# A fused attention and product-key expert kernel: W_up kept in SBUF, one-hots in rings of 64-token blocks, and the four gate blocks in one stage behind queries, picks and scores

## Chip, cores and metric

One core of one Trainium2 chip. The metric is the device time of one execution in microseconds (us), lower is better. Before the change it is 3835.45 us, the median of three runs (3822.84 to 3841.05).

## What is computed

Input is x of 2 sequences x 4096 tokens x 256 features, float32. An attention-like layer comes first (running sums over the sequence, gates, a layer norm and a projection), then a product-key mixture of experts with 8 heads:

```python
x = x + _layernorm(_L0_attn_ref(_layernorm(x), ...))
...
q = (x @ Wq + bq).reshape(B, S, 8, 64)          # x is the layer norm of the line above
s1, s2 = q1 @ K1.T, q2 @ K2.T                   # 64 scores each, per head
v1, i1 = top_k(s1, 10); v2, i2 = top_k(s2, 10)
vals, best = top_k(v1[..., :, None] + v2[..., None, :], 10)
expert_idx = i1 * 64 + i2 at best               # 10 experts per head, of 64 x 64
h = gelu(x . W_down[expert_idx]) * softmax(vals)
out = sum over heads and experts of h * W_up[expert_idx]
x = x + _layernorm(out)
```

The change touches the second phase alone.

## The kernel before

The first phase (`attention_phase`) writes x1 to DRAM. The second (`experts_phase`) works on 32 chunks m of C = 256 tokens. It does not gather experts. It computes x . W_down for all 4096 experts, multiplies by a matrix of gates that is zero where an expert was not chosen, and multiplies by W_up. An expert's number is split into q (0 to 127) and r (0 to 31), and the gates of one token are the product of two one-hot matrices over its 80 slots (8 heads x 10): `ohq` (80 x 128) and `ohr` (80 x 32), the second scaled by the gate in a high and a low half.

Every engine has its own program, a loop over m from -3 to 32 in which stages of four chunks are interleaved by hand. Semaphores join the engines. The loop body m of each engine:

- **TensorE (PE)**: `gate_matrix(m)` (line 1044): 16 fills of a PSUM bank, 32 matmuls each, in four blocks of 64 tokens; then for p = 0 to 18 `down(m, p)` (line 1117, x times W_down for 256 experts, 12 matmuls) and `up(m, p - 3)` (line 1128, 4 matmuls, listed as 8), with `turn_gates(m + 1)` at p = 4 and `turn_x(m + 3)` at p = 16; then `queries(m + 3)` (line 1092), `sum_picks(m + 2)` (1067), `scores(m + 3)` (1102), `turn_picks(m + 2)` (1074). Gates, queries and scores share three PSUM banks in rotation (`fills`, `fill`).
- **ScalarE (ACT)**: `keep_gates(m)` copies the gate banks to SBUF (1162); then per p the `gelu` of the down results (1258) and four rows of the fourth block's one-hot (`distances`, `near`: 1237, 1245); then `turn_x`, `queries`, `turn_picks`, `scores`, and `soften(m + 2)`, an exponential between two table loads (1218, 1221).
- **VectorE (DVE)**: moments, `decode(m + 1)` (expert numbers to q and r), the top-10 lists of chunk m + 2 (`lists_first`, `lists_rest`, `pair_sums`, `pairs_top`, `pick`), then `low_gates`, `onehots(m + 1, 0)`, `onehots(m + 1, 1)`, `finish(m)` (1346, statistics of the output; waits for the last `up`), `onehots(m + 1, 2)`, `norm_out(m)` (1362), `onehots(m + 1, 3)`. One block of one-hots is an ohr compare (1306), for blocks 0 to 2 an ohq compare (1312), and two ohr products (1318, 1320).
- **GpSimd (POOL)**: `mix(m, p)`, the product of gelu and gates (1002), between `down` and `up`; `low_x` (976), reciprocal roots (983, 986), `add_input` (991).
- **SyncE (SP)**: issues every DMA. Per p a load of 512 KB of W_down, split in two parts beforehand (`load_down`, 946, three slots), and one of 256 KB of W_up (`load_up`, 952, four slots).

Each one-hot of a chunk has a place of its own, so block b waits for the matmuls of the same block one chunk earlier. The ring of loads on SP waits like this:

```python
def load_down(m, p):
    n = m * PAIRS_R + p
    if n >= WD_SLOTS:
        sp.wait_ge(down_pe, n - WD_SLOTS + 1)
...
def load_up(m, p):
    n = m * PAIRS_R + p
    if n >= 4:
        sp.wait_ge(up_pe, n - 3)
```

Before the loop the kernel splits W_down into the two parts, in 16 pieces (`high_down` on ACT, line 1251, `low_down` on GpSimd, 996) and stores them in DRAM (`keep_parts`, 924 and 927).

Of the kernel before, what the change touches and what calls it, by code (L numbers as in the profile page):

```python
# [9 lines left out]
P = 128  # L10
D = 256
# [7 lines left out]
C = 256  # L19
# [13 lines left out]
WD_SLOTS = 3  # L33
# [759 lines left out]
def experts_phase(nc, ctx, sems, chunks, x1_dram, out_dram, w, x1_written):  # L793
# [16 lines left out]
    wup = sb("b_wup", [P, 4, 2, D], F32)  # L810
# [29 lines left out]
    ohq = sb("b_ohq", [SLOTS, C, NQ], F16)  # L840
    ohr = sb("b_ohr", [SLOTS, C, 2, NR], F16)
# [176 lines left out]
    def pe_program(pe):  # L1018
# [13 lines left out]
        def gate_matrix(m):  # L1032
            for g in range(GROUPS):
                if g % BLOCK_GROUPS == 0:
                    if g // BLOCK_GROUPS == BLOCKS - 1:
                        pe.wait_ge(ohq_act_done, ACT_PARTS * (m + 1))
                    else:
                        pe.wait_ge(ohq_done, (BLOCKS - 1) * m + g // BLOCK_GROUPS + 1)
                    pe.wait_ge(ohr_lo_done, BLOCKS * m + g // BLOCK_GROUPS + 1)
                bank = fill(("gates", m, g))  # L1040
                for n in range(GROUP):
                    tok = g * GROUP + n
                    for part in range(2):
                        mm = T.matmul(bank[:, n * NR:(n + 1) * NR], ohq[:, tok, :], ohr[:, tok, part, :],  # L1044
# [572 lines left out]
```

## Time and profile before

| | |
|---|---|
| median of three runs | 3835.45 us |
| the profiled execution, its own time | 3823.96 us |
| span of its profile, first to last instruction | 3822.2 us |
| mean granted TensorE clock | 0.903 |
| PE busy | 3296.1 us, 86% |
| DVE busy | 3301.0 us, 86% |
| ACT busy | 2118.1 us, 55% |
| POOL busy | 1554.4 us, 41% |
| DMA | 486.93 MB, mean 127 GB/s |

The experts' phase begins at about 797 us. Its first gate matmul starts at 969.4 us, the last at 3751.2. Shares are of the whole span. Rows of groups of instructions give line, engine, operation, output<-inputs, shapes and count, then busy time and the mean of one in ns, then the engine's idle time just before them and what ended it. Matmuls overlap, so the durations of single ones add up to more than the time they take.

### The profile page before, as it was taken

Reading aid. Unit: us, or ns where it says so; the run is one execution under the profiler, and the core shown is the slowest. Engines: PE = TensorE matmul, PEld = TensorE weight load, DVE = VectorE, ACT = ScalarE, POOL = GpSimd, SP = SyncE. Lnnn points to the kernel's source line nnn. Section 1 sums busy time; section 2 is a strip of 40 time slices with the busy share of each in tenths; the row PEclk is TensorE's granted clock in tenths of the full one; section 3 lists DMA queues with packets and bytes.
Section 4 is the critical chain, followed back from the end, with each engine's and each line's share of the span. In section 5 each row is a group of like instructions: output and inputs, shape, how many; then the busy total and the mean of one; then the engine's idle time right before and its main releaser. Section 6 shows DMA issues by size and latency. Waiting matters only on the chain.

```text
span 3822.2 us, 91364 instructions
## 1 busy us (share of the span) xinstructions
PE 3296.1 (86%) x31732; PEld 2774.3 (73%) x31732; DVE 3301.0 (86%) x15276; ACT 2118.1 (55%) x4379; POOL 1554.4 (41%) x990
## 2 busy tenths in 40 slices
PE   5999999922799898998999899998988898988887
PEld 4666666511688788887877888887888887877777
DVE  4566666529999999999999999999999999999961
ACT  3444444414556666666666666655666666666662
POOL 1334343330244444444444444444443444444443
PEclk9999999966899988899998989999988989999988
DMA  1111111140344444444444444444444444444443
GB/s 60 56 50 50 57 55 50 34 157 34 111 159 142 142 156 142 142 157 157 155 158 144 158 150 158 150 156 142 143 154 142 150 150 156 157 152 155 152 168 136
DMA packets 205910, 486.93 MB, mean 127 GB/s; under 512 B 22041, under 2 KB 69785, under 8 KB 203164
## 3 DMA queue, kind: packets, MB, share of 16 engines
q1 hardware_dynamic: 205452, 481.08, 36.5%
q8 instruction: 255, 4.18, 0.4%
q14 instruction: 203, 1.66, 0.1%
HBM read 439.03 MB, written 25.17 MB: 121 GB/s over the span
## 4 chain that ended last, share of the span: by engine, by line
PE 62%; issue 8%; ACT 3%; POOL 1%; DVE 1%; DMA 1%; POOLq 0%; DVEq 0%
PE b_ps_a L1128 22%; PE b_ps_h L1117 21%; PE b_ps_s L1044 10%; PE b_ps_m L1067 3%; PE b_ps_s L1102 3%; PE b_ps_s L1092 3%; POOL b_hid L1002 1%; ACT L1221 1%; DMA b_wd_split<-wd_parts 1%; ACT b_score L1212 0%; ACT b_gates L1162 0%; DVE b_ohq L1312 0%; ACT L1218 0%; PE b_ps_m L1057 0%; ACT b_gate L1218 0%
## 5 line engine op out<-in xcount | busy, mean ns | idle before, releaser
L1002 POOL TENSOR_TENSOR b_hid<-b_hid,b_gates 128x512 f32<-128x512 f32 x512 | 897.5, 1755 | 1264.4 <-ACT b_hid L1258 1264.2
L1117 PE MATMUL b_ps_h<-b_xT_hi,b_wd_split 128*128 128x256 f32 x4096 | 898.7, 305 | 212.1 <-issue 206.7
L1128 PE MATMUL b_ps_a<-b_wup,b_hid 128*128 128x256 f32 x4096 | 968.1, 382 | 1.8 <-POOL b_hid L1002 1.6
L1117 PEld LDWEIGHTS b_ps_h<-b_xT_hi,b_wd_split 128*128 128x128 f32 x4096 | 710.5, 203 | 313.3 <-issue 308.8
L1128 PEld LDWEIGHTS b_ps_a<-b_wup,b_hid 128*128 128x128 f32 x4096 | 751.7, 192 | 90.7 <-POOL b_hid L1002 4.2
L1258 ACT ACTIVATE b_hid<-b_ps_h 128x512 f32<-128x512 f32 x512 | 304.7, 595 | 647.2 <-PE b_ps_h L1117 647.0
L1237 ACT ACTIVATE b_ohq<-b_q_no,b_minus_qid 80x128 f16<-80x128 f16 x2048 | 648.3, 391 | 1.0
L1117 PE MATMUL b_ps_h<-b_xT_lo,b_wd_split 128*128 128x256 f32 x2048 | 603.5, 295 | 0.0
L1044 PE MATMUL b_ps_s<-b_ohr,b_ohq 80*128 80x32 f16 x16384 | 448.2, 185 | 84.9 <-ACT b_gates L1162 54.7
L1044 PEld LDWEIGHTS b_ps_s<-b_ohr,b_ohq 80*128 80x128 f16 x16384 | 439.7, 102 | 92.0 <-ACT b_gates L1162 57.8
L1312 DVE TENSOR_TENSOR b_ohq<-b_qid,b_q_no 80x8192 f16<-80x8192 f16 x96 | 449.5, 4682 | 0.0
L1117 PEld LDWEIGHTS b_ps_h<-b_xT_lo,b_wd_split 128*128 128x128 f32 x2048 | 417.7, 204 | 1.6
L1162 ACT ACTIVATE b_gates<-b_ps_s 128x512 f32<-128x512 f32 x512 | 298.4, 596 | 143.8 <-PE b_ps_s L1044 141.8
L1245 ACT ACTIVATE b_ohq<-b_ohq,b_one 80x1024 f16<-80x1024 f16 x256 | 291.5, 1139 | 0.1
L1318 DVE TENSOR_TENSOR b_ohr<-b_ohr,b_ghi 80x2048 f16<-80x2048 f16 x128 | 247.6, 1935 | 1.1
L237 POOL TENSOR_TENSOR a_ret<-a_prod 128x512 f32<-128x512 f32 x64 | 85.0, 1328 | 324.2 <-DVE a_prod L615 324.2
L1320 DVE TENSOR_TENSOR b_ohr<-b_ohr,b_glo 80x2048 f16<-80x2048 f16 x128 | 202.3, 1580 | 4.4
L1394 DVE FIND_INDEX8 b_idx<-b_val,b_score 128x8 uint16<-128x64 f32 x1024 | 200.4, 226 | 0.0
L1379 DVE FIND_INDEX8 b_idx<-b_val,b_score 128x8 uint16<-128x64 f32 x1024 | 200.3, 227 | 0.0
L1386 DVE MATCH_REPLACE8 b_score<-b_val,b_score 128x64 f32<-128x64 f32 x1024 | 199.8, 220 | 0.0
L1067 PE MATMUL b_ps_m<-b_work,b_ident 128*128 128x160 f16 x864 | 143.3, 342 | 48.3 <-DVE b_work L1488 48.3
L477 ACT COPY a_carry<-a_ps_c 32x512 f32<-32x512 f32 x128 | 68.0, 577 | 210.8 <-PE a_ps_c L333 210.5
(186 smaller groups left out, 5321.6 us busy)
## 6 DMA issues: line engine op xcount, KB each, us to landing
b_wd_split<-wd_parts SPq DMA_DIRECT2D x512, 512.0 KB, 3.6
b_wup<-in_wup SPq DMA_DIRECT2D x512, 256.0 KB, 2.7
a_keysh<-a_key SPq DMA_DIRECT2D x16, 896.0 KB, 5.4
a_x<-in_x SPq DMA_DIRECT2D x16, 512.0 KB, 4.7
x_between<-a_y SPq DMA_DIRECT2D x16, 512.0 KB, 3.2
b_x<-x_between SPq DMA_DIRECT2D x32, 256.0 KB, 2.7
wd_parts<-b_wd_split SPq DMA_DIRECT2D x16, 512.0 KB, 2.7
b_x1t<-x_between SPq DMA_DIRECT2D x32, 256.0 KB, 4.6
```

The costliest lines, as they stand in the source:

```text
L1002: G.tensor_tensor(hid[:, p % 4, :, :], hid[:, p % 4, :, :], gates[:, 2 * p:2 * p + 2, :], ALU.mult).then_inc(mix_done, 1)
L1044: mm = T.matmul(bank[:, n * NR:(n + 1) * NR], ohq[:, tok, :], ohr[:, tok, part, :], start=part == 0, stop=part == 1)
L1067: mm = T.matmul(rows, ident16[:, :], pk[:, :, c, :], start=c == 0, stop=c == NPAIR - 1)
L1117: mm = T.matmul(hbank[p % 2][:, j * C:(j + 1) * C], a, c, start=i == 0, stop=i == len(parts) - 1)
L1128: mm = T.matmul(abank[:, t * D:(t + 1) * D], hid[:, p % 4, j, t * P:(t + 1) * P], wup[:, p % 4, j, :], start=p == 0 and j == 0 and t == 0, ...
L1162: S.mul(gates[:, :, g * GROUP:(g + 1) * GROUP], sbank[fills["gates", m, g] % 3][:, :].rearrange("p (n r) -> p r n", r=NR), 1.0 / GATE_SCAL ...
L1237: op = S.activation(ohq[:, C - BLK + i, :], q_no[0:SLOTS, :], ACT.Abs, bias=minus_qid[:, i:i + 1])
L1245: S.activation(rows, rows, ACT.Relu, bias=one[:, :], scale=-1.0).then_inc(ohq_act_done, 1)
L1258: S.activation(hid[:, p % 4, :, :], hbank[p % 2][:, :].rearrange("p (j c) -> p j c", j=2), ACT.Gelu).then_inc(gelu_done, 1)
L1312: V.tensor_tensor(ohq[:, tok, :].rearrange("p n (q s) -> p n q s", s=2), qid[:, tok, :].unsqueeze(2).to_broadcast(shape_q), q_no[0:SLOTS, ...
L1318: V.tensor_tensor(hi, lo, ghi[:, tok, :].unsqueeze(2).to_broadcast(shape), ALU.mult).then_inc(ohr_hi_done, 1)
L1320: V.tensor_tensor(lo, lo, glo[:, tok, :].unsqueeze(2).to_broadcast(shape), ALU.mult).then_inc(ohr_lo_done, 1)
```

## The change

W_up stays in SBUF (`wup` holds all 32 r), loaded once; `load_up` is gone. There are four slots for W_down in place of three. `ohq` has three places of 64 tokens in place of the whole chunk: blocks 0 and 2 share place 0, block 1 has place 1, block 3 (made by ACT) has place 2. `ohr` has two places, for even and odd blocks. `gate_matrix` and `keep_gates` work by block, and the four blocks of chunk m + 1 stand at the end of loop body m.

```diff
-WD_SLOTS = 3
+WD_SLOTS = 4
...
-    wup = sb("b_wup", [P, 4, 2, D], F32)
+    wup = sb("b_wup", [P, NR, D], F32)
...
-    ohq = sb("b_ohq", [SLOTS, C, NQ], F16)
-    ohr = sb("b_ohr", [SLOTS, C, 2, NR], F16)
+
+    ohq = sb("b_ohq", [SLOTS, 3, BLK, NQ], F16)
+    ohr = sb("b_ohr", [SLOTS, 2, BLK, 2, NR], F16)
...
+    def place(b):
+        return 2 if b == BLOCKS - 1 else b % 2
...
             sp.dma_start(wdown, w["wdown"].rearrange("(k p) r q -> p k r q", p=P)).then_inc(wdown_in, 16)
+            sp.dma_start(wup[:, :, :], w["wup"]).then_inc(wup_in, 16)
...
-                    load_up(m, p)
...
-        def gate_matrix(m):
-            for g in range(GROUPS):
-                if g % BLOCK_GROUPS == 0:
-                    if g // BLOCK_GROUPS == BLOCKS - 1:
-                        pe.wait_ge(ohq_act_done, ACT_PARTS * (m + 1))
-                    else:
-                        pe.wait_ge(ohq_done, (BLOCKS - 1) * m + g // BLOCK_GROUPS + 1)
-                    pe.wait_ge(ohr_lo_done, BLOCKS * m + g // BLOCK_GROUPS + 1)
+        def gate_matrix(m, b):
+            if b == BLOCKS - 1:
+                pe.wait_ge(ohq_act_done, ACT_PARTS * (m + 1))
+            else:
+                pe.wait_ge(ohq_done, (BLOCKS - 1) * m + b + 1)
+            pe.wait_ge(ohr_lo_done, BLOCKS * m + b + 1)
+            for g in range(b * BLOCK_GROUPS, (b + 1) * BLOCK_GROUPS):
...
             pe.wait_ge(mix_done, n + 1)
-            pe.wait_ge(wup_in[p % 4], 16 * (n // 4 + 1))
+            pe.wait_ge(wup_in, 16)
...
         for m in range(-3, chunks + 1):
-            if has(m):
-                gate_matrix(m)
             for p in range(PAIRS_R + LAG):
...
             if has(m + 2):
                 turn_picks(m + 2)
+            if has(m + 1):
+                for b in range(BLOCKS):
+                    gate_matrix(m + 1, b)
...
             if has(m + 3):
                 scores(m + 3)
+            if has(m + 1):
+                for b in range(BLOCKS):
+                    keep_gates(m + 1, b)
             if has(m + 2):
                 soften(m + 2)
...
-            if m:
-                dve.wait_ge(gates_pe, GROUPS * (m - 1) + BLOCK_GROUPS * (b + 1))
+            if n >= 2:
+                dve.wait_ge(gates_pe, BLOCK_GROUPS * (n - 1))
```

PE runs the same matmuls in the same order: what stood first in body m + 1 now stands last in body m. DVE's order is the same too, with another number to wait for ahead of line 1306. Two queues change their order.

SP, the middle of one chunk's loads (`b_wd_split` are the slots of W_down, `b_wup` those of W_up, `b_down_pe` and `b_up_pe` PE's counts). Before:

```order
L946 DMA b_wd_split<-wd_parts 128x1024 [waits b_down_pe]
L952 DMA b_wup<-in_wup 128x512 [waits b_up_pe]
L921 DMA b_x<-x_between 128x2x256 [waits a_x1_out,b_xT_pe]
L946 DMA b_wd_split<-wd_parts 128x1024 [waits b_down_pe]
L952 DMA b_wup<-in_wup 128x512 [waits b_up_pe]
L946 DMA b_wd_split<-wd_parts 128x1024 [waits b_down_pe]
L952 DMA b_wup<-in_wup 128x512 [waits b_up_pe]
L940 DMA out<-b_y 128x2x256 [waits b_res]
```

After:

```order
L924 DMA b_x<-x_between 128x2x256 [waits a_x1_out,b_xT_pe]
L950 DMA b_wd_split<-wd_parts 128x1024 [waits b_down_pe] x2
L944 DMA out<-b_y 128x2x256 [waits b_res]
L950 DMA b_wd_split<-wd_parts 128x1024 [waits b_down_pe]
L940 DMA b_x1t<-x_between 128x2x256 [waits b_res]
L950 DMA b_wd_split<-wd_parts 128x1024 [waits b_down_pe] x13
```

No load of W_down stands behind one of W_up any more; what waits for an `up` is gone from the queue.

ACT, between the scores of one chunk and the first gelu of the next (`b_gates<-b_ps_s` is keep_gates, `b_gate<-b_gate` the exponential of soften). Before:

```order
L1212 COPY b_score<-b_ps_s 128x512 [waits b_lists1,b_score_pe]
L1218 ACT_TABLE_LOAD
L1218 ACTIVATE b_gate<-b_gate 128x160 [waits b_shift]
L1221 ACT_TABLE_LOAD
L1221 ACTIVATE b_unused<-b_gelu_in 128x1 [waits b_half]
L1162 ACTIVATE b_gates<-b_ps_s 128x32x16 [waits b_gates_pe,b_mix]
L1162 ACTIVATE b_gates<-b_ps_s 128x32x16 [waits b_gates_pe] x15
L1258 ACTIVATE b_hid<-b_ps_h 128x512 [waits b_up_pe,b_down_pe]
```

After (the first two rows of keep_gates stand four times):

```order
L1209 COPY b_score<-b_ps_s 128x512 [waits b_lists1,b_score_pe]
L1159 ACTIVATE b_gates<-b_ps_s 128x32x16 [waits b_gates_pe,b_mix]
L1159 ACTIVATE b_gates<-b_ps_s 128x32x16 [waits b_gates_pe] x3
L1215 ACT_TABLE_LOAD
L1215 ACTIVATE b_gate<-b_gate 128x160 [waits b_shift]
L1218 ACT_TABLE_LOAD
L1218 ACTIVATE b_unused<-b_gelu_in 128x1 [waits b_half]
L1255 ACTIVATE b_hid<-b_ps_h 128x512 [waits b_up_pe,b_down_pe]
```

The exponential and its two table loads move from ahead of the sixteen gate copies to behind them.

## Rows read from the trace of the kernel before

**Rows 1.** Busy time by engine, steady part (window; length; PE, PEld, DVE, ACT, POOL; clock)

```profile
2000.00:2500.00 500.00, 452.08 (x4809) 402.14 (x4809) 492.43 (x2345) 305.15 (x669) 234.60 (x123) 0.91 0.43 151
```

**Rows 2.** Waits of PE and DVE, 969 us to the end (total, times, longest)

```profile
PE b_ps_h L1117 <- issue: 206.7, 212, 2.2
PE b_ps_s L1044 <- ACT b_gates L1162: 54.7, 31, 1.8
...
DVE b_stat L1346 <- PE b_ps_a L1128: 96.8, 5, 67.3
```

**Rows 3.** Timeline of SP's queue, chunk 14 (start, duration of the issue)

```profile
2260.13 0.33 SPq L952 DMA_DIRECT2D b_wup<-in_wup  x1
2260.51 0.43 SPq L946 DMA_DIRECT2D b_wd_split<-wd_parts  x1
...
2264.86 0.43 SPq L946 DMA_DIRECT2D b_wd_split<-wd_parts  x1
```

**Rows 4.** Page, DMA issues (count, KB each, median us to landing)

```profile
b_wd_split<-wd_parts SPq DMA_DIRECT2D x512, 512.0 KB, 3.6
```

**Rows 5.** Timeline of PE, first matmuls of three downs, in brackets idle before

```profile
2261.05 0.36 PE L1117 MATMUL b_ps_h<-b_xT_hi,b_wd_split 128*128 128x256 f32 x1 [0.95 <-issue]
...
2264.26 0.36 PE L1117 MATMUL b_ps_h<-b_xT_hi,b_wd_split 128*128 128x256 f32 x1
...
2268.57 0.36 PE L1117 MATMUL b_ps_h<-b_xT_hi,b_wd_split 128*128 128x256 f32 x1 [0.92 <-issue]
```

**Rows 6.** Timeline of PE, queries to the next chunk's queries

```profile
2220.05 3.62 PE L1092 MATMUL b_ps_s<-b_xT,b_wq 128*128 128x256 f32 x16
...
2231.39 2.56 PE L1044 MATMUL b_ps_s<-b_ohr,b_ohq 80*128 80x32 f16 x96
2235.77 11.28 PE L1044 MATMUL b_ps_s<-b_ohr,b_ohq 80*128 80x32 f16 x416 [1.82 <-ACT b_gates L1162]
2246.88 0.56 PE L1117 MATMUL b_ps_h<-b_xT_hi,b_wd_split 128*128 128x256 f32 x1
...
2254.85 1.89 PE L1128 MATMUL b_ps_a<-b_wup,b_hid 128*128 128x256 f32 x8
...
2309.60 2.75 PE L1092 MATMUL b_ps_s<-b_xT,b_wq 128*128 128x256 f32 x12
```

**Rows 7.** Timeline of ACT, ahead of the gate copies

```profile
2232.08 1.28 ACT L1218 ACT_TABLE_LOAD   x1
```

**Rows 8.** Timeline of DVE, finish to the next chunk's moments

```profile
2309.88 0.75 DVE L1346 BATCH_NORM_STATS2 b_stat<-b_ps_a 128x6 f32<-128x256 f32 x2
...
2310.83 1.19 DVE L1306 TENSOR_TENSOR b_ohr<-b_rid,b_q_no 80x2048 f16<-80x2048 f16 x1
...
2324.17 0.74 DVE L1411 BATCH_NORM_STATS2 b_stat<-b_x 128x6 f32<-128x256 f32 x2
```

**Rows 9.** Page, groups: busy us, mean ns of one

```profile
L1318 DVE TENSOR_TENSOR b_ohr<-b_ohr,b_ghi 80x2048 f16<-80x2048 f16 x128 | 247.6, 1935 | 1.1
...
L1320 DVE TENSOR_TENSOR b_ohr<-b_ohr,b_glo 80x2048 f16<-80x2048 f16 x128 | 202.3, 1580 | 4.4
```

**Rows 10.** The tile ohr: ns min/median/max, first and last start

```profile
L1320 DVE TENSOR_TENSOR b_ohr<-b_ohr,b_glo x128: 1220/1221/2204, 968.1 to 3746.5; 80x2048 f16<-80x2048 f16 x128
...
L1318 DVE TENSOR_TENSOR b_ohr<-b_ohr,b_ghi x127: 1208/2183/2315, 974.7 to 3744.3; 80x2048 f16<-80x2048 f16 x127
```

**Rows 11.** Timeline of PE and DVE, end of an early chunk

```profile
1144.28 1.89 PE L1092 MATMUL b_ps_s<-b_xT,b_wq 128*128 128x256 f32 x8
...
1149.62 1.22 DVE L1320 TENSOR_TENSOR b_ohr<-b_ohr,b_glo 80x2048 f16<-80x2048 f16 x1
1150.77 0.75 DVE L1346 BATCH_NORM_STATS2 b_stat<-b_ps_a 128x6 f32<-128x256 f32 x2
```

**Rows 12.** DMA issues of the start, 790 to 850 us

```profile
b_gates<-in_wdown SPq DMA_DIRECT2D x1, 4096.0 KB, 15.0
```

**Rows 13.** Timeline of DVE, finish of the last chunk but one

```profile
3733.35 0.76 DVE L1346 BATCH_NORM_STATS2 b_stat<-b_ps_a 128x6 f32<-128x256 f32 x2 [27.64 <-PE b_ps_a L1128]
```

**Rows 14.** Busy time by engine, start of a down/up stage (clock: third last)

```profile
2247.00:2252.00 5.00, 5.00 (x27) 5.00 (x26) 4.93 (x45) 2.62 (x7) 1.28 (x1) 0.52 0.24 76
```

More of the change, by code:

```diff
@@ L856, in experts_phase @@
     mbank = [ps("b_ps_m0"), ps("b_ps_m1")]
-    consts_in, wq_in, wdown_in, x1_in, x1t_in, out_done = (
-        sem(f"b_{n}") for n in ("consts_in", "wq_in", "wdown_in", "x1_in", "x1t_in", "out"))
-    wup_in = [sem(f"b_wup_in{i}") for i in range(4)]
+    consts_in, wq_in, wdown_in, wup_in, x1_in, x1t_in, out_done = (
+        sem(f"b_{n}") for n in ("consts_in", "wq_in", "wdown_in", "wup_in", "x1_in", "x1t_in", "out"))
     wd_in = [sem(f"b_wd_in{i}") for i in range(WD_SLOTS)]
@@ L904, in experts_phase @@
                 fills["score", m + 3, i] = len(fills)
+        if has(m + 1):
+            for g in range(GROUPS):
+                fills["gates", m + 1, g] = len(fills)
     filled = {n: key for key, n in fills.items()}
+    def place(b):
+        return 2 if b == BLOCKS - 1 else b % 2
     def whole_slot(n):
@@ L1030, in fill @@
             return sbank[n % 3]
-        def gate_matrix(m):
-            for g in range(GROUPS):
-                if g % BLOCK_GROUPS == 0:
-                    if g // BLOCK_GROUPS == BLOCKS - 1:
-                        pe.wait_ge(ohq_act_done, ACT_PARTS * (m + 1))
-                    else:
-                        pe.wait_ge(ohq_done, (BLOCKS - 1) * m + g // BLOCK_GROUPS + 1)
-                    pe.wait_ge(ohr_lo_done, BLOCKS * m + g // BLOCK_GROUPS + 1)
+        def gate_matrix(m, b):
[5 more added lines that the diff above has]
+            for g in range(b * BLOCK_GROUPS, (b + 1) * BLOCK_GROUPS):
                 bank = fill(("gates", m, g))
                 for n in range(GROUP):
-                    tok = g * GROUP + n
+                    tok = g * GROUP + n - b * BLK
                     for part in range(2):
-                        mm = T.matmul(bank[:, n * NR:(n + 1) * NR], ohq[:, tok, :], ohr[:, tok, part, :],
+                        mm = T.matmul(bank[:, n * NR:(n + 1) * NR], ohq[:, place(b), tok, :], ohr[:, b % 2, tok, part, :],
                                       start=part == 0, stop=part == 1)
@@ L1159, in keep_gates @@
                 act.wait_ge(wd_lo_done, PAIRS_R)
-            for g in range(GROUPS):
+            for g in range(b * BLOCK_GROUPS, (b + 1) * BLOCK_GROUPS):
                 act.wait_ge(gates_pe, GROUPS * m + g + 1)
@@ L1241, in near @@
             n = BLK // ACT_PARTS
-            rows = ohq[:, C - BLK + part * n:C - BLK + (part + 1) * n, :]
+            rows = ohq[:, 2, part * n:(part + 1) * n, :]
             act.wait_ge(distance_done, PAIRS_R * m + (part + 1) * PAIRS_R // ACT_PARTS)
@@ L1262, in act_program @@
         for m in range(-3, chunks + 1):
-            if has(m):
-                keep_gates(m)
             for p in range(PAIRS_R):
@@ L1301, in onehots @@
             dve.wait_ge(rid_done, m + 1)
-            if m:
-                dve.wait_ge(gates_pe, GROUPS * (m - 1) + BLOCK_GROUPS * (b + 1))
+            if n >= 2:
+                dve.wait_ge(gates_pe, BLOCK_GROUPS * (n - 1))
             shape = [SLOTS, BLK, NR // 2, 2]
-            hi, lo = (ohr[:, tok, part, :].rearrange("p n (r s) -> p n r s", s=2) for part in range(2))
+            hi, lo = (ohr[:, b % 2, :, part, :].rearrange("p n (r s) -> p n r s", s=2) for part in range(2))
             V.tensor_tensor(lo, rid[:, tok, :].unsqueeze(2).to_broadcast(shape),
```

16 lines of the change are left out of this document (5 added, 11 removed).

## The prediction

> **What bounds the kernel now.** I read the busy shares of a stretch of the experts' phase first, then the waits, then the order of time around one hand-over of chunks. In the stretch from 2000 to 2500 us DVE is busy for 492.43 of 500 us and TensorE (PE) for 452.08 [rows 1]. A pipelined PE can be full at 90%, so both are candidates. The waits tell more [rows 2]: DVE waits for PE five times in all, 96.8 us, and of these 67.3 and 27.64 us lie behind the last lists, where DVE has nothing else [rows 2, 13]. So in steady state DVE does not wait at all (1.9 us in three waits). Its `finish` starts at 1150.77 for chunk 1 [rows 11] and at 2309.88 for chunk 14 [rows 8]: 13 periods of **89.16 us**. PE is just as slow, for another reason: 206.7 us of idle ahead of the down matmuls, 212 times about 1 us, and 54.7 us ahead of the gate matmuls, which wait for ACT [rows 2].
>
> The 206.7 us are called "issue", but they are the supply of W_down. SP sends out the wup load at 2260.13 and behind it the wd load at 2260.51 [rows 3]. The wup load waits for an `up`, and the wd load stands behind it in SP's order, though its own slot has long been free. A wd load takes 3.6 us to land [rows 4]. PE starts a down at 2261.05 and the next at 2264.26, which is 3.75 us after the issue: just in time. The one after is at 2268.57, behind 0.92 us of idle [rows 5], 3.7 us after its own issue at 2264.86. A step of one down and one up takes 3.21 us where nothing is missing (2261.05 to 2264.26) and 4.31 us where it is.
>
> **The change, part by part.**
>
> 1. *W_up resident, four wd slots.* 512 wup loads of 256 KB go; a wd load now waits only for the down four steps earlier, some 11 us before its data are due, against 3.6 us to land [rows 4]. The idle ahead of the downs should vanish. What a whole down/up stage then takes: the first four downs from 2246.88 to 2254.85 are 8.0 us [rows 6], one up 1.7 (the row has 1.89, of which the next instruction covers the end), twelve steps of 3.21 are 38.5, the last three ups, turn_gates and turn_x 5.7. Together **53.9 us**. Now it is 62.7 us, from 2246.88 to the queries at 2309.60 [rows 6]; of the 8.8 us between, 206.7/32 = 6.5 are named idle, the rest lies in steps that the gaps stretch.
>
> 2. *The ring.* Block 2's one-hots (line 1306, b = 2) reuse the place of block 0, and now wait for the gate matmuls of block 0 of the same chunk; block 3's wait for block 1. Queued behind that wait on DVE are `norm_out`, block 3, and all the lists of the next chunk. In the old schedule DVE starts block 2 at 2310.83, 0.95 us after `finish` [rows 8], when PE is only at its queries. From the queries to the first gate matmul PE takes 2220.05 to 2231.39 = 11.3 us [rows 6], and block 0 another 3.4 us (128 of the 416 matmuls of 11.28 us are 3.5 us). If PE stayed as slow as it is, DVE would lose nearly all of that, 14 us in every chunk. It does not, if part 1 holds: PE then finishes its ups well ahead of `finish`.
>
> 3. *The loop through both engines.* From block 0 done: DVE does block 2, norm_out, block 3 (2310.83 to 2324.17 = 13.3 us [rows 8]); PE then does gate block 3 (3.6), down/up (53.9), queries to turn_picks (11.3), gate block 0 (3.4). Sum **85.5 us**. PE's blocks 1 and 2 lie beside DVE's work.
>
> 4. *DVE alone.* Its instructions are the same. But their length depends on GpSimd: of the two ohr products the first takes 1208 ns at least and 1935 on average, the second 1220 and 1580 [rows 9, 10]. Per chunk that is 4 x 0.73 + 4 x 0.36 = 4.4 us, lost where the mixes run. With a faster PE, gate block 3 ends 3.6 us after DVE's block 3, and the last up ends 57.5 us after it; DVE comes to its next block 0 about 53 us after it (85.7 less 13.3 us for the ring's part, 1 for `finish` and 18 for blocks 0 and 1). So blocks 0 and 1 fall behind the mixes. I leave 0.9 us for xT_lo and add_input and take 3.5 us off: 89.2 - 3.5 = **85.7 us**. An early chunk supports it: PE began its queries at 1144.28, 6.5 us ahead of `finish` at 1150.77 [rows 11], and the last product ran its short time there. Bounds: nothing off (the mixes, now closer together, hit other DVE work), or the full 4.4 us and more from the compares, with PE's loop at 84 us.
>
> 5. *ACT.* keep_gates now comes ahead of the exponential and its table loads. The gate matmuls' 1.82 us wait [rows 6], caused by ACT's table loads from 2232.08 [rows 7], goes; it is counted in block 0 above. The exponential is late next: it now ends some 5 us into down/up, and DVE wants it 8 us after block 3, so there is room. Nothing is added.
>
> 6. *Start.* W_up's 4 MB are loaded once, behind wdown, which took 15.0 us for as much [rows 12]. The splitting of W_down starts as before, but its stores stand behind that load; the fourth slot lets four parts go ahead (about 6 us). I take +4 us, between -4 (four slots shorten the round of splits and stores) and +12.
>
> 7. *End.* In the last two chunks DVE has no lists, and waits 27.64 us for PE [rows 13]. There PE's stage decides: 2 x 8.6 = -17 us, and the ring gives 1.5 us back in the last gate stage.
>
> The larger of the two loops, 85.7 us, goes into the sum: 29 periods x -3.46 = -100; end -15.5; the first chunk's own stage -2; start +4: **-114 us**. The profiled execution is 3823.96 us, so 3710; the median shown, 3835.45, is 11.5 us above it, so **3721 us** is my prediction against the median.
>
> **A rule to weigh.** In the gate stage PE already runs at 1.2 GHz and it keeps that level into the first downs: the granted clock is 0.52 from 2247 to 2252 [rows 14], and the first four downs take 8.0 us instead of 4 x 1.5 = 6.0. The change puts idle stretches of several us between gate blocks, so the climb back to 2.4 GHz could come one such stretch later, at 2 us per chunk.
> The Trainium skill, "TensorE: Matmul & The Clock Gate", section "What's actually happening", says that the throttled clock is the default and only activity releases it. By that rule the pauses speak against the change; by the row alone the stage is cold anyway and nothing is lost.
>
> **The rivals.**
> - *A slower kernel:* the 1 us gaps are not the wd loads' (a handshake with ACT or the queue itself), down/up stays at 62.7 us, and the ring's wait lands on DVE. The loop is then 13.3 + 3.6 + 62.7 + 11.3 + 3.4 = 94.3 us, 5.1 more than now: 29 x 5.1 + 6 is +154, 3989 us. It decides from a down/up stage of 57.6 us upwards. For it: the profile names no DMA for those gaps. Against it: the downs at 2264.26 and 2268.57 both start 3.7 us after their loads' issue [rows 3, 5], the landing time of 3.6. Chance 0.09.
> - *DVE gains nothing:* collisions only move, DVE's cycle stays at 88.7. 29 x -0.5 - 13.5 is -28: 3807 us. For it: mixes every 3.2 us rather than 4 under the picks and lists. Against it: the early chunk [rows 11]. Chance 0.10, of which 0.02 within 0.5%.
> - *The clock:* the loop through both is 87.5. 29 x -1.7 - 11.5 is -61: 3774 us. Chance 0.08.
> - *No difference:* the gains are eaten by the start and by jitter between two loops of equal length, 3830 us. Chance 0.03.
>
> **How the numbers follow.** The forecast has the remaining 0.70, with a range of its own of 3660 to 3755 (DVE between 83.6 and 86.8). The whole range is 3660 to 3812: it takes in the two milder rivals and leaves out the slower kernel, the null and something below. Over 0.5% is about what a measurement of this kernel can tell from no change: faster 0.86, same 0.05, slower 0.09.
>
> **What would show it.** Right: the "issue" idle ahead of the downs under 30 us in all; down/up 53 to 55 us; the ohr products mostly at 1.21 us in blocks 0 and 1; a new wait of PE's gate matmuls for DVE's one-hots, 3 to 6 us per chunk; DVE waiting for PE at the ring by under 2 us per chunk; `finish` every 85 to 87 us; DVE above 95% busy. Wrong: gaps of 1 us ahead of the downs; DVE waits of 5 us or more ahead of line 1306; a granted clock at half for more of the down/up stage; more than 10 us between the landing of wdown and the first split.

## The result and the profile after

The changed kernel takes **3709.53 us**, the median of four runs (3707.27 to 3717.1), against 3833.19 for four of the kernel before. The ratio is **0.968** (0.9655 to 0.9710). The forecast was 3721 in a range of 3660 to 3812.

| | |
|---|---|
| the profiled execution, its own time | 3710.8 us |
| span of its profile | 3709.0 us, 113.2 less than before |
| mean granted TensorE clock | 0.882 |
| PE busy | 3227.4 us, 87% |
| DVE busy | 3194.2 us, 86% |

Where the 113.2 us come from is read from the starts of `finish`, first of DVE before (chunks 0 and 29), then of DVE after:

```profile
1061.91 0.75 DVE L1346 BATCH_NORM_STATS2 b_stat<-b_ps_a 128x6 f32<-128x256 f32 x2
3650.10 0.76 DVE L1346 BATCH_NORM_STATS2 b_stat<-b_ps_a 128x6 f32<-128x256 f32 x2 [0.38 <-PE b_ps_a L1128]
```

```profile
1063.39 0.75 DVE L1344 BATCH_NORM_STATS2 b_stat<-b_ps_a 128x6 f32<-128x256 f32 x2
...
3557.95 0.75 DVE L1344 BATCH_NORM_STATS2 b_stat<-b_ps_a 128x6 f32<-128x256 f32 x2
...
3629.01 0.76 DVE L1344 BATCH_NORM_STATS2 b_stat<-b_ps_a 128x6 f32<-128x256 f32 x2 [16.54 <-PE b_ps_a L1124]
3701.85 0.76 DVE L1344 BATCH_NORM_STATS2 b_stat<-b_ps_a 128x6 f32<-128x256 f32 x2 [56.09 <-PE b_ps_a L1124]
```

The first `finish` is 1.5 us later. The 29 periods up to chunk 29 take 2494.56 us in place of 2588.19, **86.02 each in place of 89.25**: -93.6. From there to the end it is 151.05 us (3557.95 to 3709.0) in place of 172.1: -21.1. Together 1.5 - 93.6 - 21.1 = -113.2.

The waits of PE, then those of DVE, over the experts' phase (total, times, longest). They answer to [rows 2]:

```profile
PE b_ps_s L1040 <- issue: 239.1, 80, 5.2
PE b_ps_h L1113 <- ACT b_hid L1255: 10.1, 31, 0.6
PE b_ps_h L1113 <- issue: 3.9, 3, 2.3
```

```profile
DVE b_ohr L1304 <- PE b_ps_s L1040: 11.5, 10, 2.2
```

The idle ahead of the downs has fallen from 206.7 us to 3.9, and the 54.7 us behind ACT are gone. In their place PE has 239.1 us ahead of gate matmuls, 7.7 per chunk. The new wait on DVE for the ring is 11.5 us in all.

One hand-over of chunks in PE's timeline, which answers to [rows 6]. The rows from 2180.86 are the four gate blocks, in brackets idle before:

```profile
2180.86 6.68 PE L1040 MATMUL b_ps_s<-b_ohr,b_ohq 80*128 80x32 f16 x256
2192.40 3.58 PE L1040 MATMUL b_ps_s<-b_ohr,b_ohq 80*128 80x32 f16 x128 [4.87 <-issue]
2197.91 3.58 PE L1040 MATMUL b_ps_s<-b_ohr,b_ohq 80*128 80x32 f16 x128 [1.94 <-issue]
2201.32 0.56 PE L1113 MATMUL b_ps_h<-b_xT_hi,b_wd_split 128*128 128x256 f32 x1
2209.34 1.89 PE L1124 MATMUL b_ps_a<-b_wup,b_hid 128*128 128x256 f32 x8
2254.74 3.62 PE L1088 MATMUL b_ps_s<-b_xT,b_wq 128*128 128x256 f32 x16
```

The down/up stage is 2201.32 to 2254.74, 53.4 us with the turns. PE's two idle stretches, ahead of blocks 2 and 3, are its waits for the one-hots: in the mean of the chunks each block starts 0.1 us after DVE's last product for it. Its idle moved from inside the down/up stage, where it made the loop longer, to places where it waits for DVE.

The busy time in the stretch that [rows 1] show before, same columns:

```profile
2000.00:2500.00 500.00, 452.16 (x5285) 419.96 (x5284) 490.76 (x2628) 324.51 (x710) 184.68 (x128) 0.87 0.32 109
```

The two products of [rows 9], in the groups of instructions:

```profile
L1316 DVE TENSOR_TENSOR b_ohr<-b_ohr,b_ghi 80x2048 f16<-80x2048 f16 x128 | 189.6, 1481 | 1.1
...
L1318 DVE TENSOR_TENSOR b_ohr<-b_ohr,b_glo 80x2048 f16<-80x2048 f16 x128 | 158.3, 1236 | 4.4
```

DVE is still busy all the time (490.76 of 500), and its periods are shorter because its instructions are: the high product took 1935 ns on average and takes 1481, the low one 1580 and now 1236. The wide compare of ohq fell from 4682 to 4436. Per chunk 4 x 0.45 + 4 x 0.34 + 3 x 0.25 = **3.9 us**. DVE's whole busy time fell by less, 106.8 us or 3.3 per chunk, because some of its other work now meets GpSimd more often: the wide product of the picks (L1488 before, L1486 after) takes 3316 ns on average in place of 3067.

**A stall that the prediction had not read from the profile of before.** Half of the periods (14 of 29) are 85.2 or 85.3 us, ten are over 86.5, up to 89.2. In most of the long ones PE stops inside a gate block. PE in chunk 2:

```profile
1163.20 3.15 PE L1040 MATMUL b_ps_s<-b_ohr,b_ohq 80*128 80x32 f16 x112 [1.27 <-issue]
1169.33 0.59 PE L1040 MATMUL b_ps_s<-b_ohr,b_ohq 80*128 80x32 f16 x16 [2.97 <-issue]
```

The block's one-hots are there, since its first 112 matmuls have run; the last 16 come 3 us late. SP's queue at that time:

```profile
1160.79 0.39 SPq L944 DMA_DIRECT2D out<-b_y  x1
1161.22 0.47 SPq L950 DMA_DIRECT2D b_wd_split<-wd_parts  x1
1161.73 0.45 SPq L940 DMA_DIRECT2D b_x1t<-x_between  x1
1162.23 0.47 SPq L950 DMA_DIRECT2D b_wd_split<-wd_parts  x1
```

The store of the output waits for `add_input`, two loads of W_down stand behind it, and when it goes, 1.5 MB go out at once. Eight such stops, most of 2 to 3 us, make 18.7 us.

The kernel before has such stops too. There are ten of them over 0.8 us, 12.6 us together, inside its gate blocks and away from the fills of a bank, where PE could wait for ACT. They did not lie on its path, since DVE alone set its period. One of them, in chunk 3, before:

```profile
1258.65 1.25 PE L1044 MATMUL b_ps_s<-b_ohr,b_ohq 80*128 80x32 f16 x40 [1.23 <-issue]
```

### The profile page after: what moved, and what is told of

Its sections match the earlier page's. It is cut to its first block and busy times, and to the rows that moved or that the text cites. A ratio compares the mean times of both kernels' runs of the same rounds, so it can differ in the third digit from the quotient of the medians.

```text
span 3709.0 us, 90949 instructions
## 1 busy us (share of the span) xinstructions
PE 3227.4 (87%) x31732; PEld 2785.6 (75%) x31732; DVE 3194.2 (86%) x15276; ACT 2119.9 (57%) x4379; POOL 1343.9 (36%) x990
## 5 line engine op out<-in xcount | busy, mean ns | idle before, releaser
L999 POOL TENSOR_TENSOR b_hid<-b_hid,b_gates 128x512 f32<-128x512 f32 x512 | 760.8, 1487 | 909.6 <-ACT b_hid L1255 909.1
L1124 PE MATMUL b_ps_a<-b_wup,b_hid 128*128 128x256 f32 x4096 | 955.7, 379 | 0.0
L1113 PE MATMUL b_ps_h<-b_xT_hi,b_wd_split 128*128 128x256 f32 x4096 | 929.2, 312 | 14.4 <-ACT b_hid L1255 10.1
L1124 PEld LDWEIGHTS b_ps_a<-b_wup,b_hid 128*128 128x128 f32 x4096 | 743.6, 190 | 84.0
L1040 PE MATMUL b_ps_s<-b_ohr,b_ohq 80*128 80x32 f16 x16384 | 447.0, 183 | 239.4 <-issue 239.1
L1310 DVE TENSOR_TENSOR b_ohq<-b_qid,b_q_no 80x8192 f16<-80x8192 f16 x96 | 425.8, 4436 | 0.0
L980 POOL TENSOR_SCALAR b_rstd<-b_mv 128x2 f32<-128x2 f32 x64 | 34.7, 543 | 683.7 <-DVE b_mv L1292 683.7
L1304 DVE TENSOR_TENSOR b_ohr<-b_rid,b_q_no 80x2048 f16<-80x2048 f16 x128 | 188.8, 1475 | 11.5 <-PE b_ps_s L1040 11.5
L1316 DVE TENSOR_TENSOR b_ohr<-b_ohr,b_ghi 80x2048 f16<-80x2048 f16 x128 | 189.6, 1481 | 1.1
```

The costliest lines, as they stand in the source:

```text
L999: G.tensor_tensor(hid[:, p % 4, :, :], hid[:, p % 4, :, :], gates[:, 2 * p:2 * p + 2, :], ALU.mult).then_inc(mix_done, 1)
L1040: mm = T.matmul(bank[:, n * NR:(n + 1) * NR], ohq[:, place(b), tok, :], ohr[:, b % 2, tok, part, :], start=part == 0, stop=part == 1)
L1113: mm = T.matmul(hbank[p % 2][:, j * C:(j + 1) * C], a, c, start=i == 0, stop=i == len(parts) - 1)
L1124: mm = T.matmul(abank[:, t * D:(t + 1) * D], hid[:, p % 4, j, t * P:(t + 1) * P], wup[:, 2 * p + j, :], start=p == 0 and j == 0 and t == 0 ...
L1310: V.tensor_tensor(ohq[:, place(b), :, :].rearrange("p n (q s) -> p n q s", s=2), qid[:, tok, :].unsqueeze(2).to_broadcast(shape_q), q_no[0 ...
```

## The experiments

Two theories stood against each other at first. **A:** the gain is the order on SP's queue alone (the W_down loads no longer stand behind those of W_up); residency and ring serve only to allow it, or add nothing. **B:** the new order of gates, picks and exponential on PE and ACT gives a good part. A second question was what bounds the kernel at 85.2 us, a third what the stops are.

The kernel before is not equally fast on all chips: its medians beside these runs are 3870.54 (e1 to e4), 3875.5 (e0, e9, e6, e7) and 3834.55 (e5, e8, e11, e12), each of seven runs. The change hardly differs (3709.53 in the result and 3706.74 in e0, the one run of it beside the others). Every ratio is to the kernel before of its own group. Where e3, e4, e5, e8 and e11 are set against the change or against each other across groups, it is by their mean periods; the change has 86.02 in one trace and 85.90 in the other.

**e1, the order on SP alone.** The kernel before, with each W_down load one step earlier than the W_up load it stood behind:

```diff
                 if has(m):
-                    load_down(m, p)
+                    if p == 0:
+                        load_down(m, p)
+                    if p + 1 < PAIRS_R:
+                        load_down(m, p + 1)
                     load_up(m, p)
```

> The kernel before with one thing changed: on SP's queue each W_down load is issued one step earlier, ahead of the W_up load it stood behind. No residency, no ring, no fourth slot, ACT's order as before. Theory (the 1 us gaps are the W_down loads held up behind the W_up loads, and a faster PE takes DVE out of GpSimd's mixes): the idle ahead of the downs falls from 206.7 to under 30 us, down/up from 62 to 54 us, and DVE alone decides at 85 to 86 us per chunk, so 3705 to 3730 us, level with the change. Rival (the gaps are a handshake or DMA traffic, which only residency takes away): down/up stays near 62 us and the time within 0.5% of before.

Measured: 3703.21 us, ratio 0.9564 (0.9522 to 0.9607). The waits of PE:

```profile
PE b_ps_s L1047 <- issue: 158.5, 70, 5.2
PE b_ps_s L1047 <- ACT b_gates L1165: 54.9, 31, 1.8
PE b_ps_h L1120 <- issue: 16.3, 35, 1.0
```

These few lines give as much as the whole change. The 206.7 us ahead of the downs are 16.3, the down/up stage is 53.9 us, the mean period 85.76. The 54.9 us behind ACT are still there and cost nothing. Theory A holds, and the reading that named no DMA but found the loads' landing time behind each gap [rows 3 to 5] is confirmed.

**e2, the ring and the new order without residency.** The change, with W_up again in four slots, three slots for W_down, and load_up behind load_down:

```diff
-WD_SLOTS = 4
+WD_SLOTS = 3
...
-    wup = sb("b_wup", [P, NR, D], F32)
+    wup = sb("b_wup", [P, 4, 2, D], F32)
...
                     load_down(m, p)
+                    load_up(m, p)
```

> The change without its supply part: W_up again in four slots loaded per step behind the W_down load, three W_down slots; the ring of one-hots, the gate blocks and ACT's order stay. Theory (the ring closes a loop through both engines, 13.4 + 3.6 + down/up + 11.2 + 3.4 us): with down/up at 62 us the loop is 93.6 us, DVE waits ahead of line 1306's counterpart by about 4 to 6 us per chunk, and the time is 3930 to 3980 us, slower than before. Rival (the ring costs nothing and the gain of the change comes from ACT's order): 3800 to 3835 us.

Measured: 4017.27 us, ratio 1.0385 (1.0337 to 1.0434). DVE's waits:

```profile
DVE b_ohr L1311 <- PE b_ps_s L1047: 231.1, 31, 13.6
```

This is the slower rival, made real. With down/up at 63.7 us the loop's formula gives 13.4 + 3.6 + 63.7 + 11.3 + 3.4 = 95.4, and the mean period is 95.76. The ring with the new order, but without residency, costs 3.9%; only a quick down/up stage makes it harmless. The direction is as expected, the size was put too low: 4 to 6 us of DVE's wait per chunk and 3930 to 3980 us, against 7.5 us (231.1/31) and 4017. Part of that is the chip, on which the kernel before takes 3870.54.

**e3, the store and the residual load three steps later:**

```diff
-                if p == 1 and has(m - 1):
+                if p == 4 and has(m - 1):
                     store(m - 1)
-                if p == 2 and has(m):
+                if p == 5 and has(m):
                     load_residual(m)
```

> The change, with the output store and the residual load of a chunk issued three steps later (p = 4 and 5 in place of 1 and 2), so that no W_down load stands behind the store's wait. Theory (about one chunk in four takes 3 us longer because PE's instruction fetch, 16 KB for 128 matmuls, stands behind the burst of loads that leaves SP when the store's wait ends, in the middle of the last gate block): the long gate blocks go, the period falls from 86.0 on average to the 85.2 that most chunks take, and the time by 20 to 28 us, to 3682 to 3690. Rival (the long chunks come from somewhere else, such as TensorE's clock): same as the change within 5 us.

Measured: 3692.39 us, ratio 0.9542 (0.9501 to 0.9583). In the trace the mean period is 85.24, and only one is over 86 (86.07). The profiled execution took 3682.67 us, the three others 3691.57 to 3693.6, so the time lies 2 us above what was expected and the period where it was. SP's queue in chunk 2:

```profile
1164.68 0.44 SPq L944 DMA_DIRECT2D out<-b_y  x1
1165.87 0.32 SPq L950 DMA_DIRECT2D b_wd_split<-wd_parts  x1
1166.24 0.49 SPq L940 DMA_DIRECT2D b_x1t<-x_between  x1
```

When the store's turn comes its data are ready, nothing piles up behind it, and PE has no stop over 0.8 us inside a block. With the burst gone the stops are gone; e5, below, has a smaller burst and smaller stops. DVE waits at the ring once in all, 2.2 us.

**e4, the exponential ahead of the gate copies again:**

```diff
+            if has(m + 2):
+                soften(m + 2)
             if has(m + 1):
                 for b in range(BLOCKS):
                     keep_gates(m + 1, b)
-            if has(m + 2):
-                soften(m + 2)
```

> The change with ACT's exponential and table loads ahead of the gate copies again, as before. Theory (gate block 0 takes 5.3 us rather than 3.4, and in the change block 0 is on the loop through both engines, because DVE's block 2 waits for it): 1.9 us per chunk, 29 chunks, +45 to +60 us, 3755 to 3770 us. Rival (DVE alone decides, the loop has room): within 10 us of the change.

Measured: 3744.98 us, ratio 0.9677 (0.9636 to 0.9719). Waits of PE and of DVE:

```profile
PE b_ps_s L1040 <- ACT b_gates L1159: 55.5, 31, 1.8
```

```profile
DVE b_ohr L1304 <- PE b_ps_s L1040: 43.7, 25, 4.1
```

The same 1.8 us that cost e1 nothing go into the ring's loop here. The mean period is 87.09 us, 1.07 above the change's 86.02, less than 1.8. The rest comes back in the first downs: from the start of the first down to the first up it is 7.45 us in the mean of the chunks, 8.10 in the change, and 1.8 - 0.65 = 1.15.

The reason is ACT. A down writes one of two PSUM banks, so the third waits for the first gelu and the fourth for the second. In the change the exponential and its table loads stand between the last gate copy and the first gelu. ACT in the chunk shown above, whose first down starts at 2201.32:

```profile
2203.79 1.28 ACT L1218 ACT_TABLE_LOAD   x1
...
2205.19 0.58 ACT L1255 ACTIVATE b_hid<-b_ps_h 128x512 f32<-128x512 f32 x1
...
2207.13 0.58 ACT L1255 ACTIVATE b_hid<-b_ps_h 128x512 f32<-128x512 f32 x1
```

The second gelu ends at 2207.71, and the fourth down starts 0.14 us later. So it is in 25 of 32 chunks of the change (31 of 32 in e3), and in those 25 the first four downs take 8.00 to 8.06 us, wherever TensorE's clock rises. With the exponential first, ACT does the first gelu 2.9 us after the first down's start in place of 3.8. One such chunk of e4, ACT, then PE:

```profile
2216.82 0.60 ACT L1255 ACTIVATE b_hid<-b_ps_h 128x512 f32<-128x512 f32 x1 [1.85 <-PE b_ps_h L1113]
```

```profile
2214.17 0.56 PE L1113 MATMUL b_ps_h<-b_xT_hi,b_wd_split 128*128 128x256 f32 x1
...
2220.99 1.89 PE L1124 MATMUL b_ps_a<-b_wup,b_hid 128*128 128x256 f32 x8
```

ACT waits for the down here, and the four downs take 6.8 us; the change has 2201.32 to 2209.34 = 8.0. The clock's share is small: its lower level ends 3.4 us after the first down starts in e4, 3.7 in the change and in the kernel before (means of 26 chunks). ACT's new order pays only because of the ring, and it is not free: it takes 1.8 us out of the loop at gate block 0 and puts 0.65 back in at the first downs. The direction is as expected, the size smaller (3755 to 3770 us expected).

**e0, the change once more, and e9, both edits of SP's order in the kernel before** (e1's and e3's together):

> The change itself once more, on the chip of this call, as the measure for the three others. 3700 to 3715 us if its time depends little on the chip; up to 1% more if it follows the kernel before, which took 3870 us on the chip of the last call.

> The kernel before with two changes on SP's queue alone: each W_down load ahead of the W_up load it stood behind, and the output store and residual load at p = 4 and 5. Theory (DVE alone decides, PE's fetch stalls are what is left): the mean period falls to 85.3 us and the time to 3675 to 3690 us, level with the change plus the late store. Rival (with twice the loads in flight the stalls stay): within 5 us of the 3703 us of the kernel with the first of the two alone.

Measured: e0 3706.74 us, ratio 0.9562 (0.9530 to 0.9594), mean period 85.90; e9 3700.59 us, ratio 0.9548 (0.9515 to 0.9580), mean period 85.75. The two intervals overlap: an edit of some lines on SP does what residency, ring and new order do. e9 misses its own theory, 85.3 us and 3675 to 3690: the theory took PE's stops to be what is left in e1, and neither trace has one over 0.8 us inside a gate block. The late store adds nothing to e1. With it the kernel with the ring is 0.5 us per chunk quicker than the order alone (85.24 against 85.75); on the one chip that ran both, e3 takes 3692.39 us and e1 3703.21, and the intervals of the two ratios overlap.

**e6 and e7, the mixes almost taken away.** Both have GpSimd's mix cut to 16 of its 512 columns (so the product with the gates is left out for the other 496), e6 on top of e3, e7 on top of e9:

```diff
-            G.tensor_tensor(hid[:, p % 4, :, :], hid[:, p % 4, :, :], gates[:, 2 * p:2 * p + 2, :], ALU.mult).then_inc(mix_done, 1)
+            G.tensor_tensor(hid[:, p % 4, 0, 0:16], hid[:, p % 4, 0, 0:16], gates[:, 2 * p, 0:16], ALU.mult).then_inc(mix_done, 1)
```

> The change plus the late store, with GpSimd's product of gelu and gates cut from 512 columns to 16 of 512: the rest of the hidden values goes on without its gates. It takes most of GpSimd's time beside DVE away and leaves the order of all engines. Theory (two loops of the same length, 85.2 us: DVE's own work, of which some 4 us are collisions with GpSimd, and the ring's loop through PE): DVE's own work falls to 81 to 82 us, but the ring's loop holds the period at 84.5 to 85.2 us, and 2 to 4 us per chunk appear as DVE's wait for gate block 0; 3655 to 3685 us. Rival (DVE's own work alone decides): period 81 to 82 us, 3570 to 3590 us.

> The same cut of GpSimd's product, in the kernel before with both changes of SP's queue and no ring. Theory: no loop couples DVE to gate block 0, so the collisions' whole price shows: period 81 to 82.5 us (DVE 81, or PE at 11.2 + 17.5 + 53.6 = 82.3), 3565 to 3605 us. Rival (collisions cost DVE next to nothing, the earlier gain came from elsewhere): period 84.5 to 85.2.

Measured: e6 3686.49 us, ratio 0.9508 (0.9476 to 0.9540), mean period **85.25**; e7 3600.56 us, ratio 0.9290 (0.9259 to 0.9321), mean period **82.47**. DVE's waits in e6, then e7's busy time in the same stretch, and its group of a wide product of the picks:

```profile
DVE b_ohr L1304 <- PE b_ps_s L1040: 80.0, 30, 3.4
```

```profile
2000.00:2500.00 500.00, 475.80 (x5429) 439.02 (x5428) 493.38 (x2675) 336.06 (x740) 109.31 (x133) 0.90 0.50 165
```

```profile
L1491 DVE TENSOR_TENSOR b_work<-b_work,b_cid 128x4320 f16<-128x4320 f16 x30 | 72.3, 2409 | 1.0
```

The same group in e9, where the mixes are whole:

```profile
L1491 DVE TENSOR_TENSOR b_work<-b_work,b_cid 128x4320 f16<-128x4320 f16 x30 | 101.3, 3375 | 1.0
```

Without the ring DVE gets 3.3 us per chunk back (85.75 to 82.47); the product of L1491 takes 2409 ns in place of 3375. With the ring DVE gets nearly as much and then waits: 80.0 us in 30 waits, 2.7 per chunk, and the period stays. So the change has **two loops of almost the same length**: DVE's own work, which fills the period in e3 (one wait at the ring), and the loop through the ring, 13.4 + 3.5 + 53.5 + 11.3 + 3.4 + 0.1 = 85.2 us, which holds it in e6 and e8. In the mean of the chunks DVE starts block 2 of the one-hots 0.14 us after the last matmul of block 0, in e3 as in e6 and e8, so the ring's loop has no slack in any of them. Why DVE's own work is 85.2 with the ring and 85.75 without it (e1, e9) was not taken apart.

**e5, three slots for W_down in the change** (`WD_SLOTS = 3`, nothing else):

> The change with three W_down slots in place of four. Theory (with the W_up loads gone a load leaves three steps ahead, 8 us against 3.6 to land, so the fourth slot is worth nothing in the loop and at most some us at the start): within 8 us of the change's 3707. Rival (the fourth slot carries part of the gain): idle ahead of the downs above 50 us, 3730 us or more.

Measured: 3697.52 us, ratio 0.9643 (0.9623 to 0.9663), which is 9.5 us below 3707 and so better than expected. Idle ahead of the downs is 0.2 us. The mean period is 85.37 against 85.90 and 86.02 with four slots, and the stops over 0.8 us are three, 3.1 us together. The fourth slot is worth nothing in the loop; it does harm there, some 0.6 us per chunk. It lets one more load into the burst behind the store. In chunk 2 three slots send the store, one load of W_down and the residual from 1167.10 to 1168.04, 1.0 MB in place of 1.5, and the next load of W_down at 1177.08; PE stops at the same matmul 112 for 1.05 us in place of 2.97. The fourth slot shortens the start: ACT's 16 casts that split W_down start from 818.7 to 849.6 us here and from 817.0 to 843.0 in the change, 5 us less. Over the whole kernel three slots look no worse and probably better, by 9 us across two chips.

**e8, less work on DVE, with the ring.** e3, with `low_gates` (1.7 us of DVE per chunk) moved to GpSimd behind the mix of step 7:

```diff
                     mix(m, p)
+                if p == 7 and has(m + 1):
+                    low_gates(m + 1)
...
-                low_gates(m + 1)
                 onehots(m + 1, 0)
```

> The change plus the late store, with low_gates moved from DVE to GpSimd behind mix 7. It takes 1.7 us per chunk from DVE outside the ring's loop. Theory (the ring's loop of 85.2 us holds): period 85.2 us, 3680 to 3697 us, the same as with the late store alone, and some 1.5 us per chunk of new DVE wait for gate block 0. Rival (DVE's own work decides): period 83.5, 3635 to 3650 us.

Measured: 3692.31 us, ratio 0.9630 (0.9608 to 0.9652), mean period 85.27 against e3's 85.24.

```profile
DVE b_ohr L1313 <- PE b_ps_s L1049: 20.2, 30, 2.2
```

DVE waits at the ring in every chunk, 0.7 us each where 1.5 was expected, and nothing is gained: the ring's loop holds the period.

**e11 and e12, less work on DVE, and GpSimd's `add_input` away from DVE's fourth block.** Both have e8's `low_gates` and take `add_input` out of the one-hots of chunk m + 1, to behind the mix of step 2 of the next chunk; e11 on e8, e12 on e9, so without ring and residency:

```diff
+                if p == 2 and has(m - 1):
+                    add_input(m - 1)
...
                 root(1, m)
-                add_input(m)
```

> As the kernel with low_gates on GpSimd, and GpSimd's add_input moved behind mix 2 of the next chunk, so that it no longer holds up DVE's fourth block by 1 us, which lies inside the ring's loop. Theory: the loop falls from 85.2 to about 84.2 us, the time by 25 to 35 us below the kernel without this move, 3650 to 3670 us. Rival (the loop has another member that sets it): no difference between the two.

> No ring and no residency: the kernel before with SP's two changes, low_gates on GpSimd and the late add_input. Without the ring's loop DVE's own work decides: 85.7 us less 1.7 and 1.0, and perhaps 0.5 back for collisions that move: period 83 to 83.5 us, 3615 to 3640 us, faster than the change and than every kernel with the ring. Rival (PE's own order, 11.2 + 17.5 + 54 = 82.7 us, or collisions that move eat it): 3660 us or more.

Both miss their theories. Measured: e11 3741.59 us, ratio 0.9755 (0.9733 to 0.9776), mean period 86.96; e12 **3653.92 us, ratio 0.9521 (0.9497 to 0.9546)**, mean period 84.23. Of e11 PE's waits, then SP's queue in one chunk, then PE at the down that needs the load of 2225.60:

```profile
PE b_ps_h L1123 <- issue: 58.9, 38, 3.2
```

```profile
2217.14 0.32 SPq L950 DMA_DIRECT2D b_wd_split<-wd_parts  x1
2225.17 0.39 SPq L944 DMA_DIRECT2D out<-b_y  x1
2225.60 0.47 SPq L950 DMA_DIRECT2D b_wd_split<-wd_parts  x1
```

```profile
2229.70 0.36 PE L1123 MATMUL b_ps_h<-b_xT_hi,b_wd_split 128*128 128x256 f32 x1 [1.90 <-issue]
```

e11 shortened the ring's part as meant, from 13.4 to 12.4 us, and lost 2.6 us in the down/up stage (56.1). The store at step 4 now waits for the later `add_input`, no load of W_down leaves between 2217.14 and 2225.60, and the down starts 4.1 us after the issue. It is the fault of the kernel before, made anew by the experiment, and it shows again as "issue". The loop's formula gives 12.4 + 3.6 + 56.1 + 11.3 + 3.4 = 86.8.

e12 in the same stretch of 500 us:

```profile
2000.00:2500.00 500.00, 467.84 (x5263) 429.95 (x5260) 493.53 (x2623) 330.84 (x728) 208.45 (x138) 0.90 0.48 162
```

DVE bounds it (493.53 of 500) and PE keeps up. It gains 1.5 us per chunk over e9, where 2.2 to 2.7 were expected (3615 to 3640 us): part of what left DVE may come back as collisions with GpSimd's added work, but that was not taken apart. It has the shortest time of all kernels here that do the whole computation, 1.2% below e5 and 1.0% below e8 on one chip. It beats the kernel before there, and the change as it ran on other chips (3706.74 and 3709.53), without keeping W_up in SBUF.

Residency without the ring was not tried. In the plan of the change the ring makes the room for it: by the shapes in the diff the one-hots shrink by 32 KB per partition, W_up grows by 24, and the fourth slot takes 4.

## Why the prediction was right

**The direction and the mechanism held**, by the steps of the prediction, part 5 excepted:

- *Part 1, supply of W_down.* Idle ahead of the downs under 30 us: 3.9. Down/up 53.9 forecast, 53.5 measured in the mean of the chunks. e1 shows that SP's order is enough for it.
- *Part 3, the loop through both engines.* 85.5 forecast, 85.2 measured in the chunks without a stop. e2 and e11 changed terms of the sum, and the period followed it; e6 and e8 took work from DVE beside it, and the period stayed.
- *Part 4, DVE alone.* Forecast 3.5 us per chunk back from the collisions, with bounds of nothing and 4.4. Measured 3.9 by the means of the one-hots' instructions, 3.3 by DVE's whole busy time, and 89.25 - 85.76 = 3.5 by the periods of e1, where DVE alone decides. In blocks 0 and 1 the high product now takes 1.31 and 1.25 us on average (2.26 and 2.12 before), the low one 1.25. The high product of block 3, beside `add_input`, keeps its 2.15 (1.22 in e11 and e12, where `add_input` is elsewhere): that is the 0.9 us that the prediction left standing. e7 shows that the collisions left cost another 3.3 us.
- *Part 2, the ring's wait.* Forecast under 2 us per chunk: 11.5 us in ten waits, 0.4 per chunk.
- *Part 6, the start.* +4 forecast; the first gate matmul moves from 969.4 to 973.4 us. That it fits so well is luck, since in e0, the same kernel, it starts at 970.8. e5 gives the worth of the fourth slot at the start, 5 us against an estimate of 6; what it costs in the loop was not foreseen.
- *Part 5, ACT.* "Nothing is added" did not hold. The late exponential holds up the first gelu, and through it the fourth down; e4, without it, has 0.65 us less there. No sum shows it, because the prediction took 8.0 us for the first four downs from the rows of before and they are 8.1 now. DVE also waits for the exponential seven times, 8.2 us in all, and did not before.

**The size of the gain came out right by errors that cancel.** Between the profiled executions -114 us were forecast (3710) and -113.2 measured (3710.8). The forecast period of 85.7 us meant DVE at 85.7 and the ring's loop at 85.5. Both are 85.2, and the long periods, which stand in no step of the prediction, give 0.8 us back (23.7 us in 29 periods, of which PE's stops are 18.7): the mean is 86.02. The sum of -100 for the 29 periods came out as -93.6, and the end made up for it. The 11.5 us between 3721 and the median of 3709.53 are the distance that the prediction added from the profiled execution before to its median; the change's profiled execution lies at its median.

**Two terms were off.** *The end:* -15.5 forecast, -21.1 measured. The term counted two down/up stages at 8.6 us. From `finish` of chunk 29 to that of chunk 30 it is 71.06 us in place of 83.25 (3733.35 [rows 13] less 3650.10): -12.2; the last is 72.84 in place of 81.65, -8.8. The second is the term. The first holds 3 us more, because PE no longer starts its gate matmuls behind `finish`, but is ahead of it and begins that chunk's downs 17.9 us after it in place of 21.0. *PE's wait for one-hots:* 3 to 6 us per chunk forecast, 7.7 measured. The prediction's own loop held the right number: from the start of block 0 to the end of block 3 it has 3.4 + 13.3 + 3.6 = 20.3 us, of which the matmuls are 2.56 + 11.28 = 13.8 [rows 6]; 6.5 are left, and the stops bring 18.7/31 = 0.6; another 0.6 stays open.

**The rivals.** The slower kernel did not occur, but e2 shows its price: 3989 us against 3835.45, a ratio of 1.040, where e2 has 1.0385. "DVE gains nothing" fell with the products' means. *The clock* fell too. In the first downs after the gate stage, where [rows 14] show 0.52 before, it now is (clock third last):

```profile
2198.00:2203.00 5.00, 5.00 (x136) 5.00 (x136) 4.86 (x30) 3.25 (x5) 0.96 (x2) 0.50 0.63 218
```

TensorE is at its lower level, 1.2 GHz, as before. The first four downs take 2201.32 to 2209.34 = 8.0 us, and 8.1 in the mean of the chunks, 7.8 before, where the rival had 2 us more. Even these 0.3 us are not the clock's alone, since the fourth down waits for ACT (e4). e1 and e9 have like pauses, 2.9 and 1.8 us ahead of blocks 2 and 3, and ACT's old order, and take 7.9 and 8.0. The mean granted clock falls from 0.91 to 0.87 in the stretch mostly because the lower level now lasts 20.0 us per hand-over in place of 15.1 (means of 26 chunks): the gate stage spans 20.6 us with its pauses, not 15.5 (2231.39 to 2246.88 [rows 6]).
The Trainium skill, "TensorE: Matmul & The Clock Gate", section "What's actually happening", has the throttled clock as the default, released by activity; the trace doesn't contradict it, but pauses in a stage that is throttled anyway cost at most 0.3 us per chunk here.

## What to carry to other kernels

Ask of each idle stretch named "issue" when the load that it may need was issued, and what stood ahead of that load in the order of its queue. Moving it ahead of a wait for another engine cost four lines here and was worth what a rebuilt buffer plan gave. A ring or a shared buffer closes a loop through two engines: add up that loop before and after the change, for as long as it is the longest, less work on either engine buys nothing (e6, e8), and every small wait in it counts (e4). A queue that stores results behind a slow producer delays every load behind it (e3, e11): put the store where its data are surely ready. More slots let more loads pile up behind such a store: the fourth one cost more in the loop than it gave at the start (e5). And an instruction moved off one wait can hold up another: read what stands behind it on its own engine (e4).

## What the runs showed of the hardware, unexpected

**PE can stop in the middle of a block, with its data there, when a burst of loads goes out.** Six of the eight stops of the change fall at the same matmul of the same chunks in its other trace, e0 (chunk 2 at matmul 112 of the last block, chunk 7 at 118, chunk 12 at 123). The DMA queues from 1162 to 1166 us, and from 1166 to 1169.4 (packets, MB, share of 16 engines):

```profile
q1 hardware_dynamic: 670, 1.26, 97.8%
```

```profile
q1 hardware_dynamic: 68, 0.21, 15.5%
q8 instruction: 1, 0.02, 2.0%
```

While the burst fills the engines there is no instruction packet; when it ends one of 0.02 MB comes, and PE goes on at 1169.33. At the other stops such a packet comes too: in all eight of the change and all ten of the kernel before, a 16 KB packet of this queue ends 1.2 to 1.6 us before PE goes on. That PE lacked its next instructions is argued from this; that the burst causes the stops of the change is shown by e3 and e5, where it is spread or smaller.

**GpSimd and DVE delay each other by whole instructions.** With the mixes cut to 16 columns, the picks' product takes 2409 ns in place of 3375, and the period without the ring 82.47 us in place of 85.75. In the other direction, the low half of x on GpSimd (shortest, median, longest in ns; e6, then the change):

```profile
L973 POOL TENSOR_TENSOR b_xT_lo<-b_xT,b_xT_hi x32: 1263/4774/4807, 850.7 to 3437.0; 128x512 fp32r<-128x512 f32 x32
```

```profile
L973 POOL TENSOR_TENSOR b_xT_lo<-b_xT,b_xT_hi x32: 1266/1708/5471, 849.2 to 3457.0; 128x512 fp32r<-128x512 f32 x32
```

An instruction of 1.27 us takes 4.8 where it meets DVE's compare of 4.4 us (mean of L1310 4436 ns, above). In e6 it starts 0.8 us behind the compare and ends 1.1 us after it.
The Trainium skill, "SBUF — State Buffer", section "SBUF: two separate sides", describes a port pair that either engine holds for a whole instruction while the other is blocked, also where a DVE operation reads two inputs from SBUF; the traces agree.
